# Four more low parts of the first batch's expert units computed on GpSimd, with their gated product in SBUF

## The reference, cut to what matters

```python
x = x + attn(cond(x, cond_1024), w_qkv, w_out)          # 16 heads, rope, causal softmax
# experts, on x:
for e in range(2):  shared += (silu(x @ s_w1[e].T) * (x @ s_w3[e].T)) @ s_w2[e].T
for e in range(8):  routed += gelu(x @ r_w1[e].T) @ r_w2[e].T * gates_full[:, e:e+1]
x2 = (shared / 2 + routed) / 4
# zones, on x2: three of eight per batch, chosen by a small router
x = x + x2 + sum_z w_z * (gelu(x2 @ Wa[z]) @ Wb[z])
```

## Time and profile before

| | before |
|---|---|
| median of 3 runs | 180.12 us (178.88 to 180.81) |
| profiled execution, time / span | 179.45 us / 177.6 us |
| PE busy | 168.0 us, 95% of the span |
| DVE busy | 139.3 us, 78% |
| ACT busy | 135.1 us, 76% |
| POOL busy | 93.2 us, 52% |
| granted TensorE clock | 1.00 |

### The profile page before, as it was taken

One profiled execution on the slowest core, in us unless ns is written; L12 is line 12 of the kernel. 1 busy time (PEld: TensorE's weight loads), 2 busy tenths in 40 slices (PEclk: granted clock), 3 DMA queues, 4 the chain that ended last, 5 costly groups with the idle time before them and its releaser, 6 DMA issues.

```text
span 177.6 us, 3278 instructions
## 1 busy us (share of the span) xinstructions
PE 168.0 (95%) x944; PEld 117.5 (66%) x944; DVE 139.3 (78%) x445; ACT 135.1 (76%) x224; POOL 93.2 (52%) x116
## 2 busy tenths in 40 slices
PE   6899998899999999989999999978999999999992
PEld 2766675565757666653658768846777877788881
DVE  5598989989898899980697989897798748647561
ACT  3559258687879898889644887935889999999970
POOL 5507187996355968778422522005569931777000
PEclk9999999999999999999999999999999999999999
DMA  4824685676657667340111899960770000001001
GB/s 141 302 45 100 182 204 159 227 274 208 191 187 216 178 191 189 116 135 26 59 55 33 231 334 345 347 182 8 213 262 0 0 4 0 0 2 59 0 4 59
DMA packets 15349, 24.28 MB, mean 137 GB/s; under 512 B 2844, under 2 KB 4828, under 8 KB 15308
## 3 DMA queue, kind: packets, MB, share of 16 engines
q1 hardware_dynamic: 14532, 23.29, 43.2%
q10 hardware_dynamic: 800, 0.79, 1.5%
HBM read 18.71 MB, written 5.27 MB: 135 GB/s over the span
## 4 chain that ended last, share of the span: by engine, by line
PE 58%; DVE 9%; ACT 5%; DMA 3%; issue 2%; POOL 2%; DVEq 0%; ACTq 0%
PE psum L1568 11%; PE psum L1570 10%; PE psum L1569 10%; PE psum L1495 8%; PE psum L1435 7%; PE psum L1471 5%; DMA t_stacked<-scratch 2%; ACT t_probs L1133 2%; PE psum L1475 2%; PE psum L1448 1%; DVE t_raw L950 1%; ACT t_q_pad L1183 1%; PE psum L1480 1%; DVE t_raw L954 1%; DMA scratch<-t_o_sb 1%
## 5 line engine op out<-in xcount | busy, mean ns | idle before, releaser
L798 DVE CUSTOM_DVE_ANT_0 psum<-psum,t_causal 128x128 f32<-128x128 f32 (+3 forms) x128 | 58.6, 527 | 4.1 <-PE psum L1435 3.7
L1133 ACT ACTIVATE t_probs<-psum 128x1024 f32<-128x1024 f32 (+2 forms) x48 | 41.2, 884 | 9.7 <-PE psum L1471 7.6
L1435 PE MATMUL psum<-t_stacked,t_q_pad 96*128 96x256 f32 (+2 forms) x104 | 33.9, 385 | 0.2
L692 POOL TENSOR_SCALAR_AFFINE_SELECT t_probs<-t_probs 128x512 f32<-128x512 f32 x32 | 21.0, 667 | 11.3 <-ACT t_probs L1133 10.8
L970 DVE SCALAR_TENSOR_TENSOR t_q_pad<-psum,t_zw_all,t_q_pad 128x512 fp32r<-128x512 f32 x24 | 17.8, 748 | 9.8 <-ACT t_q_pad L1181 9.4
L1435 PEld LDWEIGHTS psum<-t_stacked,t_q_pad 96*128 96x128 f32 x104 | 18.6, 189 | 9.8 <-DVE t_row_max L798 7.7
L1167 ACT ACTIVATE psum<-psum 128x512 f32<-128x512 f32 x40 | 23.5, 586 | 0.5 <-DVE t_q_pad L973 0.2
L720 POOL TENSOR_TENSOR t_q_pad<-t_raw,t_q_pad 128x512 fp32r<-128x512 f32 x8 | 10.3, 1293 | 21.6 <-ACT t_q_pad L1183 21.6
L1495 PE MATMUL psum<-t_probs,t_v_all 128*32 128x512 f32 (+3 forms) x256 | 20.6, 439 | 0.0
L798 DVE DVE_READ_ACCUMULATOR2_ANT t_row_max<- 128x1 f32 x128 | 18.2, 142 | 0.0
L1181 ACT ACTIVATE t_q_pad<-psum,t_zw_all 128x512 fp32r<-128x512 f32 x24 | 16.5, 689 | 1.0 <-PE psum L1570 0.3
(11 more groups left out here) (234 smaller groups left out, 370.7 us busy)
## 6 DMA issues: line engine op xcount, KB each, us to landing
t_stacked<-scratch SPq DMA_DIRECT2D x16, 256.0 KB, 5.8
t_probs<-in_L_ffn_Wa SPq DMA_DIRECT2D x2, 1024.0 KB, 12.9
scratch<-t_o_sb SPq DMA_DIRECT2D x7, 256.0 KB, 2.0
t_raw<-in_experts SPq DMA_DIRECT2D x7, 256.0 KB, 3.0
t_stacked<-scratch SPq DMA_DIRECT2D x9, 192.0 KB, 2.8
t_q_pad<-scratch SPq DMA_DIRECT2D x28, 48.0 KB
scratch<-t_dn_hi SPq DMA_DIRECT2D x2, 512.0 KB, 3.3
t_q_two<-scratch SPq DMA_DIRECT2D x5, 192.0 KB, 2.6
```

The lines of the kernel that those rows point to most:

```text
L692: last = G.affine_select(out=tri, in_=tri, compare_op=ALU.is_ge, fill=0.0, base=0, pattern=[[0, HG], [1, P]], channel_multiplier=-1)
L798: last = V.tensor_tensor_reduce(scores, scores, causal[:, S - width:S], 1.0, 3 * BIG, ALU.add, ALU.max, row_max[s][:, qb, j:j + 1])
L1133: A.activation(o, scores, ACT.Exp, scale=float(1.0 / np.sqrt(np.float32(HD)))).then_inc(exp_done, 1)
L1435: last = T.matmul(bank[:, o:o + width], q_pad[s][0:TOP, j, qb * P:(qb + 1) * P], stacked[0:TOP, n, 0:width], start=True, stop=True)
```

## The change

```diff
-LO_POOL = [*range(0, 4), *range(12, 16)]
+LO_POOL = [*range(0, 4), 5, 7, 9, 11, *range(12, 16)]
@@ POOL
             for i in LO_POOL:
-                if i == EXP_UNITS:
+                if i == 9:
                     pool.wait_ge(x1_hi_ready, B)
                     G.tensor_tensor(x1_lo[:, 1, :], ...)
@@ DVE, finish_hidden, routed units
-                    V.tensor_tensor(hidden_of(i), hidden_of(i), gate_of[w],
+                    V.tensor_tensor(hidden_of(i), pair[:, 1, :], gate_of[w],
@@ ACT, activate
-                o = act_out[r] if kind == "shared" else hidden_of(i)
+                o = act_out[r] if kind == "shared" else pair_of(i)[:, 1, :]
```

## The result

| | before | changed |
|---|---|---|
| median, 22 runs each | 180.30 us (178.58 to 182.71) | 178.71 us (177.84 to 181.89) |
| ratio, 95% interval | 1 | 0.9945 (0.9918 to 0.9971) |
| profiled execution, time / span | 179.45 / 177.6 us | 177.84 / 175.8 us |
| DVE busy, instructions | 139.3 us, 445 | 137.1 us, 441 |
| POOL busy, instructions | 93.2 us, 116 | 98.7 us, 120 |

A forecast was written before the change was run, and what follows sets the result against it. PE, busy 168.0 of 177.6 us, was taken as the bound, so only its waits could give time. Sum: -1.75 (up(14)) + 0.35 (zone logits) + 0 (POOL, forms) = -1.40 us, 180.12 to 178.7 us; range 177.6 to 180.2.

The forecast's parts named there:

- Up(14)'s wait: PE's wait at up(14)'s second bank for DVE's low part of unit 11 goes: 1.75 us gained on PE.
- Up(13)'s wait: PE's 0.51 us wait at up(13)'s second bank for unit 10's low part, not in the list, stays.
- What the copy's chain gives back: ACT's gates copy, behind activate(14), moves only 1.40 us earlier, as do the zone logits; PE waits 0.35 us longer there.
- The sign that was to show it: In the profile, PE waits about 0.35 us longer ahead of the zone logits, near 127.8.
- POOL's bill: Four subtractions on POOL take 1.29 us instead of DVE's 0.68, all under cover: cost 0.
- The new forms: GELU into PSUM, product into SBUF, ACT's copy from SBUF: taken as 0, at most 0.16 us of loss.
- DVE and POOL side by side: In the gates, POOL's unit 11 subtraction could hold DVE's L900 by 0 to 0.11 us; taken as 0.
- Rival B: POOL gets SBUF before L891 in the gates, holding DVE 1.2 us and delaying the copy: 179.9 us, chance 0.17.
- Rival C: Low parts alternating between DVE and POOL set the pace of units 5 to 11, 0.61 us each: 182.5 us, chance 0.06.

The follow-up runs named there:

- e1: Changed kernel with the edit kept for unit 11 alone (units 5, 7, 9 back on DVE); ratio 0.9926 to the kernel before, gain 1.65 us.
- e2: Changed kernel with only units 5, 7 and 9 on POOL, unit 11 back on DVE; ratio 0.9994 to the kernel before, gain 0.00 us.
- e4: Changed kernel with unit 10 on POOL too; ratio 0.9936 to the kernel before, gain 1.53 us.
- e5: Changed kernel with all eight routed units of batch 0 (4 to 11) on POOL; ratio 0.9973 to the kernel before, gain 0.95 us.
- f1: e4 with one operand each of L891 and L900 in PSUM; ratio 0.9927 to the kernel before, gain 2.00 us.
- g1: e5 with one operand each of L891 and L900 in PSUM; ratio 0.9956 to the kernel before, gain 1.45 us.
- f3: f1 with ACT's first zone router tanh one step earlier; ratio 0.9885 to the kernel before, gain 2.47 us.
- h2: f3 with units 5, 7 and 9 back on DVE, a repeat run; ratio 0.9918 to the kernel before, gain 2.42 us.
- f2: Changed kernel with one operand each of L891 and L900 in PSUM; ratio 0.9913 to the kernel before, gain 1.70 us.

## Why the prediction was right, point by point

- **The number.** 178.7 us was forecast and 178.71 us is the median, but that closeness is luck to half a us, since both medians scatter. The forecast gain was 1.40 us or 0.78%; the ratio gives 0.55% (0.29% to 0.82%), which is 1.0 us (0.5 to 1.5), and the aligned profiles give 1.41 us.
- **Up(14)'s wait, 1.75 us.** From the first bank's last matmul to the second bank's last took 2.45 us and takes 0.69 us (118.31 to 119.00): 1.76 us. e1 and e2 show that the whole gain hangs on unit 11.
- **Up(13)'s wait stays.** It does, 0.51 us both times.
- **What the copy's chain gives back, 0.35 us.** Counted from L829 (the profiles' offset is 0.39 us), the copy moved from 22.90 to 21.52 us, 1.38 us against 1.40 forecast, and the zone logits from 29.70 to 28.30 us, 1.40 as forecast. The sign that was to show it is only in part as described: PE's gap ahead of the logits grew by 0.24 us (from 0.59 to 0.83 us), not by 0.35. The other 0.11 us of PE's lead had gone before, at down(14); see the last point. As the logits wait for the tanh, the sum is the same. The copy sits behind activate(14) as it was said to, at 0.52 and 0.50 us.
- **POOL's bill.** Unit 7 ended at 108.83 + 1.30 = 110.13 us (110.5 forecast, less the offset 110.1), DVE waited 0.3 us for it, x1's low part ended at 111.36 us where up(12) asked at 112.89. No matmul waits for any of them; the one wait of PE for L720, 0.2 us at about 100 us, is there in both kernels. Nothing to pay, as forecast. Units 7, x1 and 9 on POOL:

```profile
108.83 1.30 POOL L720 TENSOR_TENSOR t_q_pad<-t_raw,t_q_pad 128x512 fp32r<-128x512 f32 x1 [3.04 <-ACT t_q_pad L1183]
110.08 1.28 POOL L712 TENSOR_TENSOR t_stacked<-t_x,t_stacked 128x512 fp32r<-128x512 f32 x1
111.33 1.29 POOL L720 TENSOR_TENSOR t_q_pad<-t_raw,t_q_pad 128x512 fp32r<-128x512 f32 x1
```

- **The new forms.** The product into SBUF takes 0.69 us and the high part from SBUF 0.60 to 0.62 us. As taken.
- **DVE and POOL side by side.** L900 kept its 0.20 us although POOL's row ends 0.1 us into it. That part of the sum was 0, as taken. The Trainium skill's page "SBUF — State Buffer", section "Who interferes with whom", was weighed there: by it, as the prediction read it, L900 would have been held for 0.11 us, and here it was not, by the profile's times. In every larger overlap the trace agrees with that page, for a held DVE too: 0.72 us for 0.19 in e4, 0.81 and 0.75 for 0.20 in e5, 1.82 for 0.69 in f1. The small one doesn't contradict it either. In the held 32-column rows of e4, e5 and g1 DVE's end lies 0.05 to 0.07 us behind POOL's, and L900, not held, ends 0.10 us behind it. So a hold would not show in a meeting this late: the term is 0, where the prediction had 0 to 0.11 us. L891, POOL and L900 in the changed kernel:

```profile
116.22 0.19 DVE L891 TENSOR_TENSOR psum<-t_eq 128x32 f32<-128x32 f32 x1
...
117.64 0.20 DVE L900 TENSOR_TENSOR psum<-t_s_sel,t_scale_s 128x32 f32<-128x32 f32 x1
```

```profile
116.44 1.30 POOL L720 TENSOR_TENSOR t_q_pad<-t_raw,t_q_pad 128x512 fp32r<-128x512 f32 x1 [3.83 <-ACT t_q_pad L1183]
```

- **Rival B** was a mechanism that exists and did not strike: L891 started 0.22 us ahead of POOL (116.22 and 116.44). e4 is the case in which it strikes, and there it eats nearly all of the gain of the next unit.
- **Rival C** did not strike even with eight units on POOL. Its chain, one engine's low part waiting for the other's, costs 0.3 us once, inside DVE's idle time.
- **Not foreseen:** the second meeting of the two engines, at x2's low part, which now holds POOL for 0.35 us (2.90 against 2.55 us). POOL's low part of unit 14 is late by it, and the weights of down(14) wait for it. It takes 0.11 us of PE's lead (from 1.73 to 1.62 us, counted from L829); this lies ahead of PE's wait for the zone logits, which is shorter by as much, and costs nothing here. In the list of waits of the changed kernel, 118 to 176 us:

```profile
PEld psum L1568 <- POOL t_q_pad L720: 0.3, 1, 0.3
```

What stays open: the ratio's middle, 0.55%, is a quarter of a percent smaller than what the aligned stretch says, and for f3 to h2 the ratios average 0.8% where the stretch says 1.3%. The interval holds the first; whether the part ahead of L829 is on average a little longer in the changed kernels, or the profiled executions are not typical, these runs don't tell. Open too is what the hold of x2's low part costs in the versions with unit 10 on POOL, since it was not taken away in any run.

## What to carry to other kernels

In this kernel moving work off a busy engine paid only where another engine waited for that instruction, and then only until the next wait on the same side: 2.7 us of VectorE's rows went, 1.75 us of one wait went with it, and 0.35 us came back at an instruction that merely stood behind another in ScalarE's queue. Look for the one unit whose result is late by its place in the queue, move that one, and then follow the freed engine to its next wait and ask whether the thing it waits for is itself only queued badly. When GpSimd takes over work, list VectorE's instructions with both inputs in SBUF along its new places, the short ones too, and put one operand in PSUM where they meet. Go through the list again after each step: each edit moves the later meetings, as e4 and e5 showed.

## What the runs showed of the hardware

- A DVE instruction with two tensor inputs, both in SBUF, and a POOL subtraction (two SBUF inputs, 128x512) did not run together in any overlap of 0.17 us and more, whichever came first. The later one's row is longer, by 0.13 to 0.16 us less than what was left of the earlier: 32-column instructions of 0.19 to 0.20 us took 0.72, 0.75 and 0.81 us, a 512-column subtraction of 0.69 us took 1.82 us, and POOL's pair of 2.55 us took 2.90 us. With one operand in PSUM the 32-column addition took 0.19 us in the same place.
- A 32-column instruction that meets only the last 0.1 us of POOL's row shows no hold (L900 in the changed kernel, 0.20 us; L891 in e5, overlap 0.05, 0.19 us). With an overlap of 0.17 us it took 0.22 us (L900 in e4). The held ones ended 0.05 to 0.07 us behind POOL's end.
- The store of the gates (16 KB) took 1.40 to 1.42 us in the five profiles whose chain goes through it (before, changed, e1, e2, f2); the first broadcast load behind it took 3.16 to 3.45 us for the same data. In e1 and f2 the kernel's end moved with it; in e2 (3.33 us) it did not.
